# GpSimd in place of VectorE multiplies the first 512 rows of a gated cross-attention by their inverse roots

## What is computed

```
memory_proj = memory @ W_mem.T
attn = softmax(x @ memory_proj.T / sqrt(1024))
mc = attn @ memory_proj
gate = sigmoid(concat([x, mc]) @ W_gate.T + b_gate)
fused = x + gate * mc
out = fused * rsqrt(mean(fused**2, axis=-1) + 1e-6) * norm_w
```

## Time and profile before

| | us |
|---|---|
| median of 3 runs | 297.44 |
| the profiled execution | 297.36 |
| its span, first to last instruction | 295.6 |
| busy in the span: TensorE / VectorE / ScalarE / GpSimd | 289.1 / 171.1 / 161.0 / 4.3 |

### The profile page before, as it was taken

The page is one execution under the profiler, slowest core; times in us unless marked ns, Lnnn a source line. Parts: engine busy times, 40 slices in busy tenths (PEclk is TensorE's granted clock), DMA queues, the critical chain, the costliest instruction groups (busy, mean ns, idle before and its releaser), DMA issues.

```text
span 295.6 us, 4053 instructions
## 1 busy us (share of the span) xinstructions
PE 289.1 (98%) x1632; PEld 269.6 (91%) x1632; DVE 171.1 (58%) x231; ACT 161.0 (54%) x237; POOL 4.3 (1%) x11
## 2 busy tenths in 40 slices
PE   8999999999999999999999999999999999999993
PEld 8999999898998989899898989999988888889982
DVE  3657554558566585865658563424436754344893
ACT  5548444554484735649464535543545864454664
POOL 2000000000000000000000000000000000001002
PEclk9999999999999999999999999999999999999997
DMA  7999181782938759393774320177222410000235
GB/s 206 402 405 282 40 304 59 207 314 88 328 116 243 276 131 341 90 343 145 225 294 134 80 77 11 63 280 307 71 69 75 148 67 0 1 0 12 96 144 232
DMA packets 21220, 49.56 MB, mean 168 GB/s; under 512 B 2849, under 2 KB 3745, under 8 KB 21201
## 3 DMA queue, kind: packets, MB, share of 16 engines
q1 hardware_dynamic: 21200, 49.30, 50.0%
HBM read 45.75 MB, written 3.28 MB: 166 GB/s over the span
## 4 chain that ended last, share of the span: by engine, by line
PE 92%; DVE 4%; issue 1%; POOL 0%; ACT 0%; POOLq 0%; DVEq 0%; ACTq 0%
PE ps L328 65%; PE ps L422 11%; PE ps L445 9%; DVE acc L944 2%; PE ps L436 1%; PE ps L342 1%; PE ps L449 1%; PE ps L456 1%; DVE square_sum L921 1%; DVE gate L933 1%; PE ps L353 0%; POOL rms_late L1021 0%; PE ps L509 0%; PE ps L356 0%; DVE acc L979 0%
## 5 line engine op out<-in xcount | busy, mean ns | idle before, releaser
L328 PE MATMUL ps<-act_hi,w_hi 128*128 128x400 f32 (+2 forms) x264 | 78.0, 347 | 0.0
L328 PE MATMUL ps<-act_hi,w_lo 128*128 128x400 f32 (+2 forms) x264 | 77.2, 344 | 0.0
L328 PE MATMUL ps<-act_lo,w_hi 128*128 128x400 f32 (+2 forms) x264 | 77.2, 344 | 0.0
L328 PEld LDWEIGHTS ps<-act_hi,w_hi 128*128 128x128 f32 x264 | 48.4, 188 | 2.7
L328 PEld LDWEIGHTS ps<-act_hi,w_lo 128*128 128x128 f32 x264 | 49.0, 188 | 1.8
L328 PEld LDWEIGHTS ps<-act_lo,w_hi 128*128 128x128 f32 x264 | 49.0, 188 | 1.8
L788 DVE TENSOR_TENSOR w_lo<-w_stage,w_hi 128x1024 fp32r<-128x1024 f32 (+2 forms) x23 | 26.0, 1131 | 24.4 <-ACT w_hi L574 23.4
L788 DVE TENSOR_TENSOR cn_lo<-cn_stage,cn_hi 128x1536 fp32r<-128x1536 f32 (+1 forms) x16 | 23.8, 1485 | 7.0 <-ACT cn_hi L593 5.6
L788 DVE TENSOR_TENSOR ct_lo<-ct_stage,ct_hi 128x1444 fp32r<-128x1444 f32 x16 | 25.8, 1654 | 0.5 <-ACT ct_hi L585 0.5
L574 ACT ACTIVATE w_hi<-w_stage 128x1024 fp32r<-128x1024 f32 x20 | 21.0, 1055 | 6.3 <-PE ps L328 4.5
L661 ACT ACTIVATE pc<-ps,row_inv 100x512 f32<-100x512 f32 x8 | 5.5, 688 | 31.6 <-PE ps L449 31.6
(11 more groups left out here) (121 smaller groups left out, 467.5 us busy)
## 6 DMA issues: line engine op xcount, KB each, us to landing
ct_stage<-ctxT SPq DMA_DIRECT2D x16, 722.0 KB, 8.2
cn_stage<-ctxN SPq DMA_DIRECT2D x8, 768.0 KB, 5.6
cn_stage<-ctxN SPq DMA_DIRECT2D x8, 512.0 KB, 4.4
w_stage<-w_gate_x SPq DMA_DIRECT2D x8, 512.0 KB, 6.4
w_stage<-w_gate_mc SPq DMA_DIRECT2D x8, 512.0 KB, 3.5
x_again<-xT SPq DMA_DIRECT2D x1, 3200.0 KB, 11.4
cn_stage<-ctxN SPq DMA_DIRECT2D x8, 320.0 KB
acc<-xT SPq DMA_DIRECT2D x6, 400.0 KB, 7.6
```

Source lines behind the costliest of these rows:

```text
L328: done = nc.tensor.matmul(o, wgt, stream[h][part], start=first and wgt is wh and part == 0, stop=last and wgt is wl, skip_group_check=onto)
```

## The change

GpSimd makes all eight products, one after another, between its root of the first rows and its three roots of the late rows. The function `output` and its calls leave VectorE, with their two waits, for the end of the last operation's weighting and for `rms_in`, the landing of `rms_all`. GpSimd has these two waits now. Shapes, operands, the order of the products and the semaphore `out_done` stay as they were.

```diff
-            def output(k):
-
-                rows = acc[:, k, 0:FIRST].rearrange("p (i f) -> p i f", i=4)
-                nc.vector.tensor_tensor(rows, rows, rms_all.rearrange("p (f i) -> p i f", i=4),
-                                        ALU.mult).then_inc(out_done, 1)
...
-            done = 0
             for n in range(END0 + 2, LAST):
                 gate_times(n)
                 fuse(n)
                 sum_squares(n - 1)
-                if n == END0 + 3:
-                    dve.wait_ge(weighted, END0 + 1)
-                    dve.wait_ge(rms_in, 16)
-                while done < min(KD, 2 * (n - END0 - 2)):
-                    output(done)
-                    done += 1
...
             nc.gpsimd.tensor_tensor(rms[:, :], rms[:, :], minus_half[0:FC, :], ALU.pow).then_inc(rooted, 1)
+            pool.wait_ge(weighted, END0 + 1)
+            pool.wait_ge(rms_in, 16)
+            for k in range(KD):
+                rows = acc[:, k, 0:FIRST].rearrange("p (i f) -> p i f", i=4)
+                nc.gpsimd.tensor_tensor(rows, rows, rms_all.rearrange("p (f i) -> p i f", i=4),
+                                        ALU.mult).then_inc(out_done, 1)
             for i in range(NC):
```

## The result

The changed kernel takes 303.27 us (median of 4 runs, 303.11 to 303.33) against 297.48 us for the kernel before. The ratio is 1.0195, with a 95% interval from 1.0178 to 1.0212: 1.8 to 2.1% slower, right at the 2% that a measurement tells from no change. One of the four executions of the kernel before took 1629.78 us, which no trace explains; without it the median is 297.44 us. The profiled execution of the changed kernel took 303.23 us, its span is 301.4 us.

A forecast was written before the change was run, and what follows sets the result against it. TensorE bounds the kernel except at the end, where the chain of waits runs over VectorE. 297.36 + 4.8 (late sigmoid) - 0.8 (VectorE freed) + 0.8 (clock) gives 302.2, 302.1 us unrounded; 8-in-10 range 296.4 to 305.3.

The forecast's parts named there:

- Only 0.8 us could be won: At the first chunk's gate product, VectorE is late by 0.8 us, which is all that freeing VectorE can give.
- Start at 275.0 and end at 289.0: GpSimd's eight products start once `rms_all` has landed, at 275.0, and end at 289.0, with seven hold-ups of 0.4 us.
- the low end: Price of one product on GpSimd, from two reads and a write without extra for the stride: 1.2 us.
- the doubled read: Price of one product on GpSimd with only the one strided read doubled: 1.5 us.
- In turns: From 275 to 287, VectorE's two-SBUF-input instructions and GpSimd's products run one at a time; chance 0.37 with d up to 1.56.
- Sigmoid of the first chunk at F + 2.2, later by 4.8: On ScalarE, queued behind step 14's gate, addition (1.0 us) and finish (1.2): at 291.2 in place of 286.43.
- F: The time when GpSimd's eight products end, forecast as 289.0.
- The clock: between 0 and 1.6, taken as 0.8: After idling, TensorE starts its end turns and means at 1.2 in place of 2.4 GHz, adding 0.8 us.
- The sum: Whole kernel: 297.36 + 4.8 - 0.8 + 0.8 = 302.2, or 302.1 us by unrounded numbers, 1.6% slower.
- The long product: Rival: same turns on GpSimd, but each product takes over 1.56 us, so over 2% slower; 306.1 at 1.9; chance 0.28.
- d: The time of one product on GpSimd, taken as 1.4 us, between 1.2 and 1.9.

## Why the prediction was right

- *Only 0.8 us could be won.* Right: the first chunk's gate product follows its sigmoid after 0.38 us in place of 1.13, and this 0.75 is the whole gain.
- *Start at 275.0 and end at 289.0.* Measured 275.28 and 288.95, but with two errors that cancelled. A product alone is 1.50 us apart from the next, not 1.4: the factor between the low end and the doubled read was nearer to the doubled read, which gave 1.5. And a VectorE instruction holds GpSimd up for 0.22 us (1.72 - 1.50), not for 0.4. Why it is only half of its 0.45 us no run shows. That the end came out to 0.05 us was luck.
- *In turns.* Right, and what decided the sign. The expected rows of up to 1.8 us are there (1.80), and the run with one PSUM input takes them away. The Trainium skill (SBUF — State Buffer, section Who interferes with whom) says that a GpSimd instruction which reads SBUF and a VectorE instruction with two SBUF inputs share an interface, and that one waits for the other's end. The changed kernel's 1.80 against 0.46 us agrees, and so do 0.45 with an input from PSUM and 0.46 beside memsets. It does not hold in full for a GpSimd instruction with one input, which held VectorE up for 0.2 to 0.4 us of its 1.2 to 1.6 and ran beside it for the rest.
- *Sigmoid of the first chunk at F + 2.2, later by 4.8.* Measured F + 1.94, later by 4.46; this contains the 0.3 of the start. At F one instruction of step 14 was nearly through, where I had both still to come, so the step from F to the square was 0.84 in place of 1.0, and the finish took 1.1 in place of 1.2.
- *The clock: between 0 and 1.6, taken as 0.8.* This is the term that was mis-sized. It cost 1.8 us by the run with TensorE kept busy. I had doubled only the work up to the first mean. But the low clock stayed for the whole of the end, where TensorE's turns and means are now the chain: it works on them without a gap from 291.04 to 297.17, where it took 286.22 to 290.82 with gaps.
- *The sum*: 302.1 forecast, 303.27 measured. The missing 1.2 us is the stretch from the chunk's gate product to the end (2.1 in place of 0.8, so +1.3, of which the clock is shown for 1.0), less 0.3 for the sigmoid (4.46 in place of 4.8, start included), +0.1 for the gain (0.75 in place of 0.8), and 0.1 between span and median.
- *The long product* set its mark for a loss of over 2% at d = 1.56 us, and this rival did not come true: a product took 1.50, and with its turn 1.72, less than the 1.8 of the forecast. That the loss still came to 1.95% is the clock's doing. For the price of a product, the figures of the Trainium skill (GPSIMD Engine Reference, sections Elementwise — side-by-side cycle accounting and Performance pitfalls for Q7 kernels) would have given an estimate of 1.1 us dense and 1.7 strided. Measured is 1.50 strided, so the step costs less here than by the page. Dense is my estimate of 1.25 (1.47 in the turns with every fourth column, less the same 0.22); no run had a dense product alone.

## What to carry to other kernels

Before you move an elementwise operation with two SBUF inputs from VectorE to GpSimd, look at what VectorE does meanwhile. If its instructions have two SBUF inputs too, each of them waits out what is left of a GpSimd instruction, and the move can cost more of VectorE's time than it frees (here 1.35 us of waiting for 1.03 us saved). The waiting was gone where VectorE read one operand from PSUM. That it would be gone where VectorE is idle follows from this, but was not run. And where the end of a kernel is a chain over several engines, idling on TensorE can be paid twice: here it stood for 4.35 us, came back at half its clock, and the end took 1.8 us more.

## What the runs showed of the hardware

- A GpSimd multiplication by a constant, with one input, is hardly faster than the product with two: 512 columns took 1.49 us where nothing met it, against 1.54 for the strided product alone, and 384 columns 1.17.
- Such a one-input instruction on GpSimd held VectorE's instructions with two SBUF inputs up when they started in its first 0.35 us (0.46 us became 0.64 to 0.87); those that started 0.6 us or more into it ran at 0.46.
- A store of 512 pieces of 4 bytes from 128 partitions took 8.5 to 9.3 us until the queue went on; 128 pieces of 16 bytes took 1.4 to 1.9.
- TensorE's weight loads of float32 with a step of 16 bytes took 1.94 us for eight, dense ones 0.97.
- VectorE's product took 0.60 us (1.29 for a pair) with dense operands and 1.03 with one of them at a step of 16 bytes; on GpSimd the same step cost some 0.25 us of 1.5, by the estimate above.
